# A table of slots in a fused Mamba and mixture-of-experts layer: softplus one slot earlier, normalisation three earlier, the first expert tile's Y one later

## The chip, the cores and the metric

The kernel runs on one core of a Trainium2 chip. The core has five engines that each work through a list of instructions in order: TensorE (PE) multiplies matrices, VectorE (DVE), ScalarE (ACT) and GpSimd (POOL) work on elements, SyncE (SP) issues DMAs. They wait for one another by semaphores. The metric is the time of one execution on the device in microseconds (us).

## The reference, cut to what matters

The input x has 2 batches of 4096 tokens of width 256. Everything is float32.

```python
xn = layernorm(x)
# Mamba branch
r = xn * rsqrt(mean(xn * xn) + eps) * norm_w
x_s, z = split(r @ in_proj_w.T)                  # 512 channels each
u = silu(causal_conv(x_s, 4 taps) + conv_b)
dt, B, C = split(u @ x_proj_w.T)                 # 16, 16, 16
delta = softplus(dt @ dt_proj_w.T + dt_proj_b)
h[t] = exp(delta[t] * A) * h[t-1] + delta[t] * u[t] * B[t]    # 512 channels x 16 states
y = (sum over states of h * C + u * D) * silu(z)
mamba = y @ out_proj_w.T + xn
# experts: 8, two per token
w = sparse_mixer_top2(xn @ gate_w.T)
moe = sum over chosen e of w_e * ((silu(xn @ w1[e].T) * (xn @ w3[e].T)) @ w2[e].T)
out = x + mamba + moe
```

## The kernel before, in words

The tokens are cut into 32 blocks of 256, ordered by `number(j, b)`, batch 0 and 1 in turn, since the recurrence runs along a batch. One block is worked in 32 slots, `v` = 0 to 31, one for each pair of a state and a half of the channels. In every slot the engines do the following.

- POOL makes the product du * B for the slot four ahead (`make_dbu`, L475) into a ring `h` of 8 buffers. It waits until PE has transposed what was in the buffer.
- ACT makes DA = exp(delta * A) for the next slot (`make_da`, L748), two ACTIVATEs, into a PSUM tile with two buffers. So it cannot run more than two slots ahead of the scans.
- DVE runs the recurrence as two scans (`scan`, L1071), waiting for both.
- PE transposes the state of two slots before (`transpose_h`, L1305) into HT, which has two halves, so that it waits for the addition of the state before the last. DVE multiplies by C and adds it (`add_state`, L1082), four slots behind the scan.

Around this carousel stand the steps that prepare the next block and finish the one before. The table `SLOTS` says in which slot each stands; every engine walks the same 32 slots and emits the steps that are due, in the order in which its `step` function asks for them. In one slot ACT emits DA first, then the steps of expert tiles, then tanh of z, the normalisation, and so on to exp and ln. The softplus is abs (L716), exp (L722) and ln (L730) on ACT, the sums `sp0`, `sp1` on DVE (L1061), and on POOL w-1 (`wm`, L483), the correction (`corr`, L488), `delta` (L494) and `du` (L499). ACT loads a table ahead of ln and another behind it. The first DA of the next block waits for `delta`, the first product for `du`. POOL waits for the exponential (`exp_ready`) at the start of the slot of `wm`, ahead of the product of that slot.

The experts' work comes in tiles of 128 token places that share an expert, 135 in all, in the blocks 2 to 28 at 5 a block. A tile starts at the slots 4, 13, 18, 23 and 30 (`XT_UNITS`); the stages after it are offsets: transposition XT, its copy on ACT, H1 = x w1 (L1354), H3 = x w3 (L1361), tanh on ACT (L647), the product A2 on DVE (L1038), MULT with H3 on DVE (L1047), Y = ha w2 (L1368) on PE, YO on ACT (L654), and on POOL the gather of a tile (L443) and the scatter of its result (L452), both indirect DMAs. `tile_of` turns a slot into a tile.

Of the kernel before, what the change touches and what calls it, by code (L numbers as in the profile page):

```python
# [27 lines left out]
def build(nc, x, norm_w, inT_d, conv_w, conv_b, xpT_d, dtT_d, dt_b, A_log, D_par, outT_d, gwT_d, w1T_d, w2T_d, w3T_d, out):  # L28
# [12 lines left out]
    U = CH * NS // 2  # L41
# [24 lines left out]
    with ExitStack() as ctx:  # L66
        def sb(name, shape, dt=F32):
            return ctx.enter_context(nc.sbuf_tensor(name, shape, dt))
# [60 lines left out]
        delta = sb("delta", [P, 2, CH, T])  # L129
        du = sb("du", [P, 2, CH, T])  # L130
# [6 lines left out]
        cT = sb("cT", [P, 2, NT, NS])  # L137
# [100 lines left out]
        def tile_of(j, b, v, stage):  # L238

            for k in range(PER):  # L240
                at = U * (k // len(XT_UNITS)) + XT_UNITS[k % len(XT_UNITS)] + stage
                for pair in (0, 1, -1):
                    if at - 2 * U * pair == U * b + v:
                        return j - pair, k
            return None

        def tiles_at(j, b, v, stage):

            at = tile_of(j, b, v, stage)
            if at is None:  # L250
                return None
            jj, k = at
            if isinstance(jj, int) and not (J0 <= jj and (jj - J0) * PER + k < NTILES):
                return None
            return (jj - J0) * PER + k, k

        def filled(j, b, v, stage, ring=WSLOTS):

            jj, k = tile_of(j, b, v, stage)
            return (jj - J0) * (PER // ring) + k // ring + 1  # L260
# [3 lines left out]
        def add_slot(j, b, v):  # L264
# [2 lines left out]
            return at // 2 if at >= 0 and at % 2 == 0 and at // 2 < 2 * JB - 2 else None  # L267

        SLOTS = {"z0": 31, "tanh_z0": 0, "silu_z0": 1, "z1": 2, "tanh_z1": 3, "silu_z1": 4,
                 "first0": 3, "first1": 4, "y0": 4, "gate_y0": 6, "y1": 5, "gate_y1": 7, "out0": 27, "out1": 29,  # L270
                 "oacc": 17, "result": 31,
# [4 lines left out]
        XT_UNITS = (4, 13, 18, 23, 30)  # L276

        LOGITS, ROUTE = 2, 3
# [5 lines left out]
            return isinstance(j, int) and number(j, b) == 1  # L284

        INDEX, GATHER = -5, -4
        XT, XT_COPY, H1, H3, TANH, A2, MULT, Y, YO, SCATTER = 0, 1, 2, 3, 3, 4, 4, 5, 6, 8
        W1_LOAD, W3_LOAD, W2_LOAD = 4, 5, 7

        def due(name, v):  # L290
# [1193 lines left out]
```

How the kernel before makes its waits and increments, by code:

```python
def wait(eng, sem, value):  # L17
    if not isinstance(value, int) or value > 0:
        eng.wait_ge(sem, value)
# [278 lines left out]
            def load_x(j, b):  # L299
                n = number(j, b)
                sp.wait_ge(s_inT, 16)
                if isinstance(n, int) and n < 3:
                    wait(sp, s_xn, 2 * n)
                else:
                    sp.wait_ge(s_res, n - 2)
                sp.dma_start(xraw[:, :, :], x_v[b, j]).then_inc(s_x, 16)
# [1 line left out]
            def reload_x(j, b):  # L308
                n = number(j, b)
                sp.wait_ge(s_inT, 16)
                if isinstance(n, int) and n + 2 >= 2 * JB:
                    sp.wait_ge(s_res, n)
                else:
                    sp.wait_ge(s_xn, 2 * (n + 2) + 2)
                sp.dma_start(xraw[:, :, :], x_v[b, j]).then_inc(s_xres, 16)
# [1 line left out]
            def store_b(j, b):  # L318
                n = number(j, b)
                sp.wait_ge(s_xdbc, n + 1)
                sp.dma_start(b_dram[b], xdbc[R:R + NS, :]).then_inc(s_bst, 16)
# [1 line left out]
            def load_b(j, b, r):  # L323
                n = number(j, b)
                if r == 0:
                    sp.wait_ge(s_bst, 16 * (n + 1))
                wait(sp, s_dbu, 32 * n + 4 * (r + 1 - BRING))
                sp.dma_start(bbc[:, r % BRING], b_dram[b][2 * r:2 * r + 2, :].partition_broadcast(P)).then_inc(s_b[r % BRING], 16)
# [1 line left out]
            def store_out(j, b):  # L330
                sp.wait_ge(s_res, number(j, b) + 1)
                sp.dma_start(out_v[b, j], res).then_inc(s_mamba, 16)
```

## Time and profile before

| | us |
|---|---|
| median of 3 runs | 2661.89 |
| lowest, highest | 2659.11, 2669.71 |
| the profiled execution, its own time | 2653.93 |
| its span in the trace | 2652.2 |
| share busy: DVE, PE, POOL, ACT | 93%, 86%, 77%, 63% |
| mean granted clock of TensorE | 0.936 |

The span is the time from the first to the last record of the trace. The stretch from about 400 to 2400 us holds the blocks with expert tiles, and one block there looks like the next. A row of a view in order of time has the start, the duration, the engine, the line, the operation, its tiles and how many instructions were merged; what stands in brackets is how long the engine had been idle and what ended it. A scan of a slot is two instructions. In such a view the slots are found by the steps that stand in them: the A2 of a tile that starts at 18 stands in slot 22.

### The profile page before, as it was taken

The page shows a single profiled execution, that of the slowest core. Times are in us where ns is not written, and L with a number is a line of the kernel's source. Part 1 is how long each engine was busy: PE and PEld are TensorE (multiplying, and loading weights), DVE is VectorE, ACT ScalarE, POOL GpSimd, SP SyncE. Part 2 cuts the span into 40 slices and gives each one's busy share as a digit, 9 for nine tenths or more (in the row PEclk, how much of TensorE's full clock was granted, in tenths as well). Part 3 has the DMA queues.
Part 4 walks back from the last instruction along what each step waited for, and adds up shares of the span by engine and source line. Part 5 has one row for each costly group of instructions (what it writes and reads, how often), then busy time and mean ns, then how long its engine had stood idle before and what let it go on. Part 6 is the DMA issues. An engine that isn't in the chain of part 4 may idle for free. (4 is left out here: it accounts for less than half of the span.)

```text
span 2652.2 us, 47132 instructions
## 1 busy us (share of the span) xinstructions
PE 2292.8 (86%) x14442; PEld 1986.7 (75%) x14442; DVE 2459.2 (93%) x4041; ACT 1658.9 (63%) x4137; POOL 2031.0 (77%) x1607
## 2 busy tenths in 40 slices
PE   3958789899999999998999989999989899998665
PEld 2855578878787887877888877888877787887554
DVE  7679999999999999999999999999999999999997
ACT  3940566666666666666666666666666666666653
POOL 3430678888888888888888888888888888888883
PEclk7858899999999999999999999999999999999776
DMA  7216045565555555555555555555555555542451
GB/s 244 92 40 216 29 124 156 154 176 152 161 151 152 157 160 171 158 157 153 155 160 155 166 163 151 158 156 160 154 162 164 156 152 157 159 113 52 96 100 32
DMA packets 267099, 379.38 MB, mean 143 GB/s; under 512 B 21492, under 2 KB 158324, under 8 KB 266852
## 3 DMA queue, kind: packets, MB, share of 16 engines
q1 hardware_dynamic: 236196, 332.26, 40.2%
q0 software_dynamic: 28480, 43.94, 10.1%
q8 instruction: 119, 1.95, 0.3%
q14 instruction: 128, 1.05, 0.1%
q10 hardware_dynamic: 2176, 0.18, 0.1%
HBM read 332.59 MB, written 52.10 MB: 145 GB/s over the span
## 5 line engine op out<-in xcount | busy, mean ns | idle before, releaser
L475 POOL TENSOR_TENSOR h<-du,bbc 128x512 f32<-128x512 f32 x1024 | 1362.5, 1354 | 505.3 <-PE HT L1305 375.3
L1071 DVE TENSOR_TENSOR_SCAN h<-DA,carry,h 128x256 f32<-128x256 f32 x2048 | 1417.7, 734 | 91.4 <-ACT DA L748 79.0
L748 ACT ACTIVATE DA<-delta,alog 128x256 f32<-128x256 f32 x2048 | 882.6, 468 | 212.2 <-DVE h L1071 200.9
L1305 PE MATMUL HT<-ident,h 128*128 128x128 f32 x4096 | 665.8, 288 | 260.5 <-DVE yT L1082 259.1
L1305 PEld LDWEIGHTS HT<-ident,h 128*128 128x128 f32 x4096 | 496.6, 148 | 416.2 <-issue 375.2
L1082 DVE SCALAR_TENSOR_TENSOR yT<-HT,cT,yT 128x512 f32<-128x512 f32 x960 | 698.5, 728 | 3.1 <-PE HT L1305 3.1
L1354 PE MATMUL G<-xtT,W 128*128 128x128 f32 x2160 | 273.2, 281 | 0.0
L1368 PE MATMUL G<-W,fill 128*128 128x256 f32 x1080 | 271.8, 397 | 0.0
L1361 PE MATMUL G<-xtT,W 128*128 128x128 f32 x2160 | 263.4, 275 | 0.0
L1354 PEld LDWEIGHTS G<-xtT,W 128*128 128x128 f32 x2160 | 261.1, 198 | 0.0
L1361 PEld LDWEIGHTS G<-xtT,W 128*128 128x128 f32 x2160 | 252.2, 192 | 0.0
L452 POOL DMA_INDIRECT moe_dram<-W,token x135 | 217.5, 1611 | 25.2 <-issue 24.3
L1368 PEld LDWEIGHTS G<-W,fill 128*128 128x128 f32 x1080 | 205.5, 201 | 24.7
L647 ACT ACTIVATE fill<-G 128x512 f32<-128x512 f32 x135 | 80.6, 597 | 190.7 <-PE G L1354 184.6
L443 POOL DMA_INDIRECT W<-xn_dram,token x135 | 139.7, 1035 | 21.8 <-issue 16.0
L483 POOL TENSOR_SCALAR tmpA<-tmpB 128x1024 f32<-128x1024 f32 x32 | 117.2, 3663 | 30.2 <-ACT tmpB L722 30.2
L654 ACT ACTIVATE W<-G,weight 128x256 f32<-128x256 f32 x135 | 63.7, 472 | 121.0 <-PE G L1368 120.9
L1226 PE MATMUL FA<-xrT,inT 128*128 128x256 f32 x512 | 128.2, 396 | 0.0
L1378 PE MATMUL FA<-outT,zs 128*128 128x256 f32 x512 | 127.2, 394 | 0.8 <-DVE zs L1098 0.8
L1226 PE MATMUL FB<-xrT,inT 128*128 128x256 f32 x512 | 126.4, 392 | 0.8 <-ACT xrT L617 0.8
L1047 DVE TENSOR_TENSOR fill<-fill,G 128x512 f32<-128x512 f32 x135 | 92.5, 685 | 36.7 <-PE G L1361 34.4
L1260 PE MATMUL FB<-xs,cwd 128*128 128x256 f32 x512 | 121.0, 379 | 0.0
(183 smaller groups left out, 2986.6 us busy)
## 6 DMA issues: line engine op xcount, KB each, us to landing
W<-in_w_T_dram SPq DMA_DIRECT2D x405, 512.0 KB, 4.2
bbc<-b_dram SPq DMA_DIRECT2D x256, 256.0 KB, 4.3
xraw<-in_x_dram SPq DMA_DIRECT2D x64, 256.0 KB, 2.7
xn_dram<-W SPq DMA_DIRECT2D x8, 1032.0 KB, 14.0
W<-in_x_dram SPq DMA_DIRECT2D x32, 256.0 KB, 6.7
moe_dram<-fill SPq DMA_DIRECT2D x32, 256.0 KB, 4.0
out_dram<-tmpA SPq DMA_DIRECT2D x32, 256.0 KB, 2.2
out_dram<-moe_dram POOLq DMA_DIRECT2D x32, 256.0 KB, 4.4
```

Of the source, the lines that this page charges most:

```text
L443: pool.indirect_dma_start(xt[:, k % 2, :], None, xn_dram[:, :], bass.IndirectOffsetOnAxis(ap=token[:, k % META:k % META + 1], axis=0)).the ...
L452: pool.indirect_dma_start(moe_dram[:, :], bass.IndirectOffsetOnAxis(ap=token[:, k % META:k % META + 1], axis=0), yo[:, k % 2, :], None, co ...
L475: pool.tensor_tensor(h[:, v % RING], du[:, b, 2 * q:2 * q + 2, :], bbc[:, s // 2 % BRING, s % 2, :].unsqueeze(1).to_broadcast([P, 2, T]), ...
L748: i = act.activation(DA[:, v % 2, k, :], delta[:, b, c, :], ACT.Exp, scale=nega[:, c, s:s + 1])
L1071: i = dve.tensor_tensor_scan(h[:, v % RING, k, :], DA[:, v % 2, k, :], h[:, v % RING, k, :], carry[:, b, s, c:c + 1], ALU.mult, ALU.add)
L1082: i = dve.scalar_tensor_tensor(out=yT[:, b, k, :], in0=HT[:, k, :], scalar=cT[:, b, k, s:s + 1], in1=yT[:, b, k, :], op0=ALU.mult, op1=ALU ...
L1226: i = pe.matmul(dst[:, c, :], inT[:, k, at:at + P], xrT[:, b, k, :], start=(c == 0 and k == 0), stop=(k == KD - 1), skip_group_check=True)
L1305: i = pe.transpose(HT[:, k, c * P:(c + 1) * P], h[:, (2 * s + c // 2) % RING, c % 2, k * P:(k + 1) * P], ident[:, :])
L1354: i = pe.matmul(G[:, 0, f * P:(f + 1) * P], w1[:, k % WSLOTS, c, f * P:(f + 1) * P], xtT[:, c, :], start=(f == 0 and c == 0), stop=(c == K ...
L1361: i = pe.matmul(G[:, 1, f * P:(f + 1) * P], w3[:, k % WSLOTS, c, f * P:(f + 1) * P], xtT[:, c, :], start=(f == 0 and c == 0), stop=(c == K ...
L1368: i = pe.matmul(G[:, 0, 0:DM], ha[:, f * P:(f + 1) * P], w2[:, k % WSLOTS, f, :], start=(f == 0), stop=(f == IC - 1))
L1378: i = pe.matmul(FA[:, t, :], zs[:, c, t * P:(t + 1) * P], outT[:, c, :], start=(c == 0), stop=(c == CH - 1))
```

## The change

In the table `SLOTS` the exponential goes from slot 22 to 21 and the logarithm from 23 to 22; `sp0`, `sp1`, `wm`, `corr`, `delta`, `du`, `cT` and `copy_cT` go one slot up as well. The normalisation of the next block goes from 6 to 3, the second product of the input projection from 10 to 9, the second half of the output projection from 29 to 28, the result from 31 to 30. Of the expert tiles, MULT, Y and YO become offsets for each of the five tiles: the tile that starts at 4 has its MULT at 9 in place of 8, its Y at 10 in place of 9 and its YO at 11 in place of 10; the tile that starts at 23 has its Y at 29 and its YO at 30, one later each. All scatters stand one slot later. `tile_of` gets a line that takes such a tuple.

```diff
-                at = U * (k // len(XT_UNITS)) + XT_UNITS[k % len(XT_UNITS)] + stage
+                at = U * (k // len(XT_UNITS)) + XT_UNITS[k % len(XT_UNITS)]
+                at += stage[k % len(XT_UNITS)] if isinstance(stage, tuple) else stage
...
-                 "x_proj": 17, "copy_xdbc": 18, "dt": 19, "abs": 20, "exp": 22, "ln": 23, "sp0": 24, "sp1": 25,
-                 "wm": 23, "corr": 24, "delta": 26, "du": 27, "cT": 25, "copy_cT": 26}
+                 "x_proj": 17, "copy_xdbc": 18, "dt": 19, "abs": 20, "exp": 21, "ln": 22, "sp0": 23, "sp1": 24,
+                 "wm": 22, "corr": 23, "delta": 25, "du": 26, "cT": 24, "copy_cT": 25}
...
-        XT, XT_COPY, H1, H3, TANH, A2, MULT, Y, YO, SCATTER = 0, 1, 2, 3, 3, 4, 4, 5, 6, 8
+        XT, XT_COPY, H1, H3, TANH, A2, SCATTER = 0, 1, 2, 3, 3, 4, 9
+        MULT, Y, YO = (5, 4, 4, 4, 4), (6, 5, 5, 6, 5), (7, 6, 6, 7, 6)
```

The lines of the changed kernel are numbered two higher behind these. On ACT, from slot 21 to slot 24, `fill<-G` is the tanh of a tile, `tmpB<-tmpA` the exponential, `xs<-tmpB` the logarithm. Before:

```order
L748 ACTIVATE DA<-delta,alog 128x256 x2
L647 ACTIVATE fill<-G 128x512
L748 ACTIVATE DA<-delta,alog 128x256 x2
L755 COPY carry<-h 128x4
L722 ACTIVATE tmpB<-tmpA 128x1024
L748 ACTIVATE DA<-delta,alog 128x256 x2
L730 ACT_TABLE_LOAD
L730 ACTIVATE xs<-tmpB 128x4x256
L748 ACT_TABLE_LOAD
L748 ACTIVATE DA<-delta,alog 128x256 x2
```

The same stretch of ACT in the changed kernel:

```order
L750 ACTIVATE DA<-delta,alog 128x256 x2
L649 ACTIVATE fill<-G 128x512
L724 ACTIVATE tmpB<-tmpA 128x1024
L750 ACTIVATE DA<-delta,alog 128x256 x2
L757 COPY carry<-h 128x4
L732 ACT_TABLE_LOAD
L732 ACTIVATE xs<-tmpB 128x4x256
L750 ACT_TABLE_LOAD
L750 ACTIVATE DA<-delta,alog 128x256 x4
```

Two DAs stood between the tanh and the first table load and one does now; the DAs for scans 24 and 25 both stand behind the second load.

On POOL, from the slot of `wm` to the start of the next block, `h<-du,bbc` is a product for a slot four ahead, `W<-xn_dram` a gather, `moe_dram<-W` a scatter. Before:

```order
L483 TENSOR_SCALAR tmpA<-tmpB 128x1024
L475 TENSOR_TENSOR h<-du,bbc 128x512
L488 TENSOR_TENSOR tmpA<-tmpB,tmpA 128x1024
L475 TENSOR_TENSOR h<-du,bbc 128x512
L430 COPY token<-W 128x1
L475 TENSOR_TENSOR h<-du,bbc 128x512
L494 TENSOR_TENSOR delta<-delta,tmpA 128x1024
L443 DMA W<-xn_dram,token 128x258
L452 DMA moe_dram<-W,token 8320x256
L475 TENSOR_TENSOR h<-du,bbc 128x512
L499 TENSOR_TENSOR du<-delta,u 128x1024
L475 TENSOR_TENSOR h<-du,bbc 128x512 x4
```

The changed kernel, from the row behind its w-1 (now L485):

```order
L454 DMA moe_dram<-W,token 8320x256
L477 TENSOR_TENSOR h<-du,bbc 128x512
L490 TENSOR_TENSOR tmpA<-tmpB,tmpA 128x1024
L477 TENSOR_TENSOR h<-du,bbc 128x512 x2
L496 TENSOR_TENSOR delta<-delta,tmpA 128x1024
L432 COPY token<-W 128x1
L477 TENSOR_TENSOR h<-du,bbc 128x512
L501 TENSOR_TENSOR du<-delta,u 128x1024
L445 DMA W<-xn_dram,token 128x258
L477 TENSOR_TENSOR h<-du,bbc 128x512
L454 DMA moe_dram<-W,token 8320x256
L477 TENSOR_TENSOR h<-du,bbc 128x512 x4
```

Both lists end with the first four products of the next block. Between w-1 and these stand 4 products and one scatter before, and 5 products and two scatters now. The wait for the exponential stands one product ahead of w-1 in both: before, the product for slot 27, and now, that for slot 26.

On DVE, in slots 8 and 9, `fill<-fill,G` is A2 (L1038) and MULT (L1047) of the tile that starts at 4. Before:

```order
L1071 SCALAR_TENSOR_TENSOR h<-DA,carry,h 128x256 x2
L1038 SCALAR_TENSOR_TENSOR fill<-fill,G 128x512
L1082 SCALAR_TENSOR_TENSOR yT<-HT,cT,yT 128x512
L1047 TENSOR_TENSOR fill<-fill,G 128x512
L1071 SCALAR_TENSOR_TENSOR h<-DA,carry,h 128x256 x2
L1082 SCALAR_TENSOR_TENSOR yT<-HT,cT,yT 128x512
```

And in the changed kernel:

```order
L1073 SCALAR_TENSOR_TENSOR h<-DA,carry,h 128x256 x2
L1040 SCALAR_TENSOR_TENSOR fill<-fill,G 128x512
L1084 SCALAR_TENSOR_TENSOR yT<-HT,cT,yT 128x512
L1073 SCALAR_TENSOR_TENSOR h<-DA,carry,h 128x256 x2
L1084 SCALAR_TENSOR_TENSOR yT<-HT,cT,yT 128x512
L1049 TENSOR_TENSOR fill<-fill,G 128x512
```

MULT stands behind the scan and the addition of slot 9.

## Rows read from the trace of the kernel before

**Rows 1.** The page: busy time of each engine, share, instructions.
```profile
PE 2292.8 (86%) x14442; PEld 1986.7 (75%) x14442; DVE 2459.2 (93%) x4041; ACT 1658.9 (63%) x4137; POOL 2031.0 (77%) x1607
```

**Rows 2.** Waits of DVE, 800 to 2300 us: total us, times, longest us.
```profile
DVE h L1071 <- ACT DA L748: 28.7, 58, 0.6
DVE fill L1047 <- PE G L1361: 24.2, 62, 1.3
...
DVE h L1071 <- POOL h L475: 2.9, 14, 0.2
```

**Rows 3.** DVE in order of time: start, duration; in brackets the wait before.
```profile
1002.02 1.39 DVE L1071 TENSOR_TENSOR_SCAN h<-DA,carry,h 128x256 f32<-128x256 f32 x2 [0.45 <-ACT DA L748]
...
1005.83 1.39 DVE L1071 TENSOR_TENSOR_SCAN h<-DA,carry,h 128x256 f32<-128x256 f32 x2
1007.13 0.72 DVE L1082 SCALAR_TENSOR_TENSOR yT<-HT,cT,yT 128x512 f32<-128x512 f32 x1
1007.77 1.38 DVE L1071 TENSOR_TENSOR_SCAN h<-DA,carry,h 128x256 f32<-128x256 f32 x2
...
1010.79 1.39 DVE L1071 TENSOR_TENSOR_SCAN h<-DA,carry,h 128x256 f32<-128x256 f32 x2 [0.40 <-ACT DA L748]
...
1027.32 1.39 DVE L1071 TENSOR_TENSOR_SCAN h<-DA,carry,h 128x256 f32<-128x256 f32 x2 [0.19 <-POOL h L475]
...
1040.79 1.39 DVE L1071 TENSOR_TENSOR_SCAN h<-DA,carry,h 128x256 f32<-128x256 f32 x2 [0.64 <-ACT DA L748]
...
1049.01 0.69 DVE L1047 TENSOR_TENSOR fill<-fill,G 128x512 f32<-128x512 f32 x1 [0.51 <-PE G L1361]
...
1078.82 1.39 DVE L1071 TENSOR_TENSOR_SCAN h<-DA,carry,h 128x256 f32<-128x256 f32 x2 [0.45 <-ACT DA L748]
```

**Rows 4.** ACT in order of time, slots 21 to 24.
```profile
1003.00 0.60 ACT L647 ACTIVATE fill<-G 128x512 f32<-128x512 f32 x1 [1.01 <-PE G L1354]
...
1004.38 1.06 ACT L722 ACTIVATE tmpB<-tmpA 128x1024 f32<-128x1024 f32 x1
1005.34 0.86 ACT L748 ACTIVATE DA<-delta,alog 128x256 f32<-128x256 f32 x2
...
1009.89 0.87 ACT L748 ACTIVATE DA<-delta,alog 128x256 f32<-128x256 f32 x2
```

**Rows 5.** POOL in order of time, slots 26 to 8.
```profile
1019.27 1.06 POOL L443 DMA_INDIRECT W<-xn_dram,token  x1
...
1022.95 2.92 POOL L499 TENSOR_TENSOR du<-delta,u 128x1024 f32<-128x1024 f32 x1
1025.95 4.96 POOL L475 TENSOR_TENSOR h<-du,bbc 128x512 f32<-128x512 f32 x4
...
1042.56 1.27 POOL L475 TENSOR_TENSOR h<-du,bbc 128x512 f32<-128x512 f32 x1 [1.09 <-ACT carry L755]
...
1045.05 3.08 POOL L475 TENSOR_TENSOR h<-du,bbc 128x512 f32<-128x512 f32 x2
```

**Rows 6.** ACT in order of time, slots 4 and 6.
```profile
1039.52 0.47 ACT L654 ACTIVATE W<-G,weight 128x256 f32<-128x256 f32 x1 [0.48 <-PE G L1368]
...
1042.46 1.09 ACT L601 ACTIVATE tmpA<-xraw,nrs,rs 128x256 f32<-128x256 f32 x2
```

**Rows 7.** Chain of waits, slots 9 to 17: start, duration, piece.
```profile
2209.23 0.44 PE HT L1305 x4
2209.67 1.73 PE FA L1226 x8
...
2222.94 1.80 PE G L1361 x16
```

**Rows 8.** PE in order of time, slot 23.
```profile
1008.00 0.63 PE L1305 MATMUL HT<-ident,h 128*128 128x128 f32 x4 [2.25 <-DVE yT L1082]
```

**Rows 9.** One stretch: busy us (instructions) of PE, PEld, DVE, ACT, POOL; clock, DMA.
```profile
1009.00:1012.00 3.00, 3.00 (x11) 2.37 (x10) 2.60 (x5) 2.96 (x8) 3.00 (x3) 0.55 0.12 46
```

**Rows 10.** DVE in order of time, slot 27 of another block.
```profile
2249.57 0.69 DVE L1038 SCALAR_TENSOR_TENSOR fill<-fill,G 128x512 f32<-128x512 f32 x1 [1.02 <-ACT fill L647]
```

More of the change, by code:

```diff
@@ L269, in build @@
         SLOTS = {"z0": 31, "tanh_z0": 0, "silu_z0": 1, "z1": 2, "tanh_z1": 3, "silu_z1": 4,
-                 "first0": 3, "first1": 4, "y0": 4, "gate_y0": 6, "y1": 5, "gate_y1": 7, "out0": 27, "out1": 29,
-                 "oacc": 17, "result": 31,
[1 row of a table removed]
+                 "first0": 3, "first1": 4, "y0": 4, "gate_y0": 6, "y1": 5, "gate_y1": 7, "out0": 27, "out1": 28,
+                 "oacc": 17, "result": 30,
[1 row of a table added]
                  "conv0": 11, "conv1": 12, "conv2": 13, "conv3": 14, "tanh_u0": 13, "silu_u0": 14, "tanh_u1": 15, "silu_u1": 16,
[2 rows of a table removed]
[2 rows of a table added]
         XT_UNITS = (4, 13, 18, 23, 30)
```

2 rows, old and new, of the table SLOTS are left out of this document.

## The prediction

> **What bounds the kernel now.** I read the page first: DVE is busy for 93% of the span, POOL for 77%, PE for 86% [rows 1]. Busy shares do not say who is late, so next came the waits of DVE in the steady stretch, 800 to 2300 us, about 19.5 blocks: scans wait for the exponentials DA of ACT (28.7 us), the third product of an expert tile waits for PE's H3 (24.2 us), and scans wait for POOL's products only 2.9 us [rows 2]. Then I read one block in order of time. DVE starts slot 22 at 1002.02 and the next slot 22 at 1078.82, so a block lasts 76.8 us, and the reader is to see where DVE waits in it: 0.45 at scan 22, 0.40 at scan 25, 0.19 at scan 0, 0.64 at scan 6, 0.51 for H3 in slot 8 [rows 3]. These and a few smaller gaps sum to some 4 us, so a change of order can win at most about 5%.
>
> The small wait at scan 0 is the important one. It shows that POOL, though 77% busy, has no slack there: from the exponential of the softplus to the first product of the next block it works without a pause. The chain of waits says a third thing: from slot 9 to slot 17 PE is continuously busy and DVE waits for its last piece, H3 [rows 7]. So three engines take turns within one block: ACT at slots 22 to 25, POOL from there to slot 0, PE from slot 3 to slot 17. A term counts only where its engine has the turn.
>
> **The exponential and logarithm one slot earlier: ACT.** In the profile ACT works without a pause from the tanh at 1003.00 to the end of DA 25 at 1009.89 + 0.87 = 1010.76: tanh, DA 23, exp, DA 24, table load, ln, table load, DA 25 [rows 4]. The new order does the same work: tanh, exp, DA 23, load, ln, load, DA 24, DA 25. DA 25 is ready at 1010.76 again, but DA 24 only 0.87 before, at 1009.9, where it was ready at about 1006.2 before. DA has two buffers, so it cannot be made earlier. DVE wants scan 24 after scan 23 (1005.83 to 1007.13), a state addition (to 1007.77) [rows 3] and the first softplus sum, which now stands there and which I put at the 0.65 of the addition: 1008.4. The wait is 1.5 us in place of the 0.40 at scan 25, so DVE is 1.1 us late from here on. In slot 27 H3 comes relatively 0.3 later, since the second softplus sum no longer separates scans 25 and 26, and at scan 0 the old 0.2 of waiting is used up. On DVE's own path scan 0 comes 1.2 us late, at 1028.5.
>
> **The same steps on POOL.** POOL's w-1, correction, delta and du move one slot up, the scatters of the expert tiles one slot down. From the end of the exponential to the end of the product for scan 0, POOL had 6 products and one scatter beside these four passes, one gather and one token copy. In the new order the wait for the exponential stands ahead of the product for scan 26, and the scatter that was issued before that wait comes behind it, while the second scatter still precedes the product for scan 0. So 7 products and two scatters lie between. Prices: a product takes 4.96 / 4 = 1.24 us [rows 5]. A scatter: between the end of a product at 42.56 + 1.27 = 43.83 and the end of the second next at 45.05 + 3.08 = 48.13 lie 4.30 us, less two products 1.8 us. The other end is from the gather's end at 19.27 + 1.06 = 20.33 to the start of du at 22.95: 2.62 less one product, 1.4 us [rows 5]. Added work is 1.24 + 1.4 to 1.8; the exponential ends 0.87 earlier, since DA 23 no longer stands ahead of it. The product for scan 0 is ready 1.8 to 2.2 us later than 25.95 + 1.24 = 1027.19, at 1029.0 to 1029.4. That is behind the 1028.5 of DVE's own path, so POOL decides, and scan 0 starts 1.75 to 2.15 us later than in [rows 3]. I take 1.9. Behind it POOL has pauses and catches up. The gather for the fourth tile now starts behind du, at about 1024; it has to land by about 1027.6, so PE may wait some tenths there, which slot 31 hides.
>
> **Normalisation at 3.** Two ACTIVATEs, 1.09 us, move from behind DA 7 to ahead of DA 5. Scan 6 waits for DA 6 already [rows 3], and between the old and the new place of the step ACT waits only 0.48 us, for PE, ahead of YO [rows 6]. So DA 6, and with it scan 6, comes 1.09 - 0.48 = 0.6 us later. Removing it from slot 6 gives nothing, since ACT then waits for H1 anyhow.
>
> **First tile's product at 9, Y at 10.** The product ha no longer waits in slot 8: 0.51 us less on DVE. That the two do not simply add comes from PE. Its work of slots 3 to 8 depends on DVE's slot 3 and runs on. The state addition of slot 9, which releases PE's slot 9, is then about 0.5 us earlier than now; that of slot 10, which now comes behind the moved product, is back where it was (0.6 later by the normalisation, 0.5 earlier by the wait). From slot 10 on PE has the same matmuls as before (the xs product and Y swap), each with its transposes about 2.17 us [rows 7], against 1.95 of DVE. So PE reaches H3 of slot 17 within about 0.1 of where it does now. I count zero for both edits, with -0.5 and +0.6 as ends, where only one of them reaches the end. YO one slot later lies just ahead of DA 13, which is ready at 1057.5 where scan 13 wants it at 1057.6: cover is used up but nothing is lost.
>
> **Output at 28, result at 30, cT at 24, other scatters.** PE's slots 27 to 29 exchange out and Y, with room. SP's stores come one slot earlier. Zero, covered by PE's waits for state additions in slots 30 and 31.
>
> **The sum.** 135 tiles at 5 a block lie in 27 blocks: 27 x 1.9 = 51.3. The 4 other blocks with a successor have no scatters, so only ACT's 1.1 counts: 4.4. Together 55.7 us. The profiled execution took 2653.93 (span 2652.2), so it would be 2709.6; it was 8 us faster than the median of the runs, 2661.89, so for the median 2717.6.
>
> **Rivals.** (a) The clock falls once more per block. In the profile PE pauses 2.25 us before slot 23 [rows 8], and in the stretch behind it, 1009 to 1012, the granted clock is 0.55, so most of it ran at 1.2 of 2.4 GHz [rows 9]; there it costs nothing. In one block it fell later, under the first product of the tile at 23, and that tile's A2 waited 1.02 us [rows 10]; slot 27 in other blocks had no such wait. In the new order scan 24 comes 1.5 us later, so PE, which waits for the state addition behind each scan, pauses before slots 24 and 25 too, about 1 us more in all. The Trainium skill, "TensorE: Matmul & The Clock Gate", section "Part 1: The HAM clock gate", says that the array falls to 1.2 GHz after idling and returns to 2.4 GHz under sustained work; by that rule the added pause speaks for a fall at this second place, and the trace agrees as far as its one late case goes. Price: DVE's path reaches scan 0 at 1028.5 + 1.0 = 1029.5 plus up to 0.6 from H3; that is 0.3 to 0.9 behind POOL, so 2.2 to 2.8 a block, 2726 to 2742. With part of the 0.6 of the normalisation on top it is 2750. Chance 0.22. (b) The 0.5 of the moved product is kept and scatters overlap the products: 0.7 to 1.4 a block, 2685 to 2704. Chance 0.14. (c) The other side: ACT. If ACT could run ahead by 1.6 us, DA 24 would be ready by 1008.4, and the early exponential would give POOL its 0.87 while the waits of 0.40, 0.19 and 0.51 went. That is 1.1 a block, 31 us: 2631. It decides at the tanh of slot 21: it would have to start before 1001.4, but PE's H1 ends at 1003.0 and POOL must have no second scatter in the way. Chance 0.08. (d) The terms cancel, within 0.5% (about 13 us, what a measurement of this kernel can tell from no change): it needs POOL's prices to be wrong, spans there being rough, and the 0.5 to be kept. 2662, chance 0.08. My forecast has the remaining 0.48.
>
> **Numbers.** Slower: forecast, (a) and (b), 0.48 + 0.22 + 0.14 = 0.84. Same 0.08, faster 0.08. The range leaves out (c) and (d) and runs from the low end of (b), 2685, to the high end of (a), 2750.
>
> **What would show it.** Scan 24 waits about 1.5 us for DA, the wait at scan 25 is gone; scan 0 waits 0.5 to 0.9 us for POOL, and the total of DVE's waits for POOL rises from 2.9 us to over 10. The H3 wait in slot 8 is gone. A block lasts 78.7 us in place of 76.8. I would be wrong if the scan 24 wait were under 0.5 us, if scan 0 did not wait for POOL, or if the block lasted 77 us or less.

## The result, and the profile after

| | before | after |
|---|---|---|
| median, us (4 runs each) | 2664.3 | 2727.36 |
| lowest, highest | 2659.11, 2669.71 | 2724.11, 2731.28 |
| profiled execution, its span | 2653.93, 2652.2 | 2731.28, 2729.5 |
| mean granted clock of TensorE | 0.936 | 0.918 |

The changed kernel takes 1.0237 [1.0211, 1.0264] of the time, 63 us more. The forecast was 2718 with a range of 2685 to 2750. The time is inside it, but a good part of it came by another road than the forecast said: 2727 also lies in the 2726 to 2742 that I gave rival (a), the clock, and it is this rival that the profile shows at work.

The page after, to be laid beside [rows 1]. DVE works as long as before (2457 and 2459 us) in a span 77 us longer, so all of the loss is waiting; PE shows 41 us more work for the same number of instructions.

```profile
PE 2333.5 (85%) x14442; PEld 2032.4 (74%) x14442; DVE 2457.1 (90%) x4041; ACT 1658.8 (61%) x4137; POOL 2026.6 (74%) x1607
```

The waits of DVE, 800 to 2300 us (total us, times, longest), beside [rows 2]:

```profile
DVE h L1073 <- ACT DA L750: 42.9, 74, 1.5
DVE fill L1040 <- ACT fill L649: 34.4, 37, 2.1
DVE fill L1049 <- PE G L1363: 22.2, 71, 0.9
DVE h L1073 <- issue: 9.0, 6, 1.5
```

And one row of the kernel before, for the same window:

```profile
DVE fill L1038 <- ACT fill L647: 6.4, 24, 1.0
```

Three things are to be seen. The longest wait for DA is now 1.5, as forecast; the last row is the same wait at scan 24, in six blocks in which the profile names nobody for it. The second row is a wait that the forecast had only as a rival: A2, which waits for ACT's tanh of an expert tile, rose from 6.4 us (24 times, longest 1.0) to 34.4 us. And there is no row for POOL at all, where the forecast had over 10 us.

One block of the changed kernel on DVE, in order of time (start, duration, in brackets the wait ahead), beside [rows 3]: scan 22, scan 24, then slot 27's A2 and product, scan 0, scans 5 and 6, slot 9's product of the first tile, scan 22 of the next block, its scan 24 and its A2, and the scan 0 behind that.

```profile
1028.79 1.39 DVE L1073 TENSOR_TENSOR_SCAN h<-DA,carry,h 128x256 f32<-128x256 f32 x2 [0.45 <-ACT DA L750]
...
1036.78 1.39 DVE L1073 TENSOR_TENSOR_SCAN h<-DA,carry,h 128x256 f32<-128x256 f32 x2 [1.50 <-ACT DA L750]
...
1046.67 0.69 DVE L1040 SCALAR_TENSOR_TENSOR fill<-fill,G 128x512 f32<-128x512 f32 x1 [2.08 <-ACT fill L649]
...
1048.91 0.69 DVE L1049 TENSOR_TENSOR fill<-fill,G 128x512 f32<-128x512 f32 x1 [0.89 <-PE G L1363]
...
1057.88 1.38 DVE L1073 TENSOR_TENSOR_SCAN h<-DA,carry,h 128x256 f32<-128x256 f32 x2
...
1069.89 1.39 DVE L1073 TENSOR_TENSOR_SCAN h<-DA,carry,h 128x256 f32<-128x256 f32 x2 [0.43 <-ACT DA L750]
1071.72 1.39 DVE L1073 TENSOR_TENSOR_SCAN h<-DA,carry,h 128x256 f32<-128x256 f32 x2 [0.44 <-ACT DA L750]
...
1081.30 0.67 DVE L1049 TENSOR_TENSOR fill<-fill,G 128x512 f32<-128x512 f32 x1
...
1108.92 1.39 DVE L1073 TENSOR_TENSOR_SCAN h<-DA,carry,h 128x256 f32<-128x256 f32 x2 [0.45 <-ACT DA L750]
...
1116.91 1.39 DVE L1073 TENSOR_TENSOR_SCAN h<-DA,carry,h 128x256 f32<-128x256 f32 x2 [1.50 <-ACT DA L750]
...
1126.19 0.69 DVE L1040 SCALAR_TENSOR_TENSOR fill<-fill,G 128x512 f32<-128x512 f32 x1 [1.46 <-ACT fill L649]
...
1136.92 1.38 DVE L1073 TENSOR_TENSOR_SCAN h<-DA,carry,h 128x256 f32<-128x256 f32 x2
```

From scan 22 to scan 0 it takes 29.09 us here and 28.00 in the next block, where it took 25.30 [rows 3]: +3.8 and +2.7. (Over all blocks it goes in turn 28.0, 27.7, 29.1, 28.0.) From scan 0 to the next scan 22 it takes 51.04 in place of 51.50: 0.46 less. Scan 24 waits its 1.50 and scan 25 no longer waits. Slot 9's product does not wait. Scan 0 does not wait for POOL: DVE itself comes too late for that.

What made A2 late stands on PE, slots 23 to 25, in order of time (the last row is H1 of the tile that starts at 23):

```profile
1034.77 0.63 PE L1307 MATMUL HT<-ident,h 128*128 128x128 f32 x4 [2.25 <-DVE yT L1084]
...
1038.96 0.63 PE L1307 MATMUL HT<-ident,h 128*128 128x128 f32 x4 [1.61 <-DVE yT L1084]
...
1041.50 1.09 PE L1307 MATMUL HT<-ident,h 128*128 128x128 f32 x4 [1.66 <-DVE yT L1084]
1042.38 3.62 PE L1356 MATMUL G<-xtT,W 128*128 128x128 f32 x16
```

And the same stretch in windows of 3 us (busy us and instructions of PE, PEld, DVE, ACT, POOL; then the granted clock; DMA share and GB/s):

```profile
1036.00:1039.00 3.00, 1.39 (x8) 0.91 (x7) 2.22 (x4) 2.97 (x10) 2.84 (x4) 1.00 0.35 45
1039.00:1042.00 3.00, 1.34 (x9) 1.07 (x10) 3.00 (x6) 1.85 (x6) 3.00 (x3) 0.73 0.82 212
1042.00:1045.00 3.00, 3.00 (x16) 3.00 (x15) 2.59 (x5) 0.00 (x0) 3.00 (x3) 0.50 0.00 0
1045.00:1048.00 3.00, 3.00 (x19) 3.00 (x19) 1.33 (x2) 1.96 (x5) 2.92 (x4) 0.63 0.21 35
1048.00:1051.00 3.00, 3.00 (x20) 2.48 (x19) 2.11 (x5) 0.38 (x3) 2.85 (x2) 1.00 0.88 281
```

For comparison the same transposes of slot 25 and the same H1 in the kernel before:

```profile
1012.98 0.63 PE L1305 MATMUL HT<-ident,h 128*128 128x128 f32 x4 [0.44 <-DVE yT L1082]
1013.44 1.95 PE L1354 MATMUL G<-xtT,W 128*128 128x128 f32 x16
```

The pause of 2.25 ahead of slot 23 stood there before [rows 8]. Ahead of slot 24 there was none and is 1.61 now, ahead of slot 25 there was 0.44 and is 1.66 now. Both are the echo of scan 24's wait, since PE's transposes wait for the state addition that follows a scan. (In two of four blocks the clock has fallen already behind the pause of 2.25; the slower work then fills the pause ahead of slot 24, the 1.66 stays, and the clock is down a second time under H1.) The clock falls between 1039 and 1042 (0.73 in that window), is at 0.50, half of 2.4 GHz, up to 1045 and back at 1.00 from 1048, and H1 takes 3.62 us, where it takes 1.95 at full clock. The tanh and A2 hang on that H1. Over 420 to 2400 us the mean granted clock fell from 0.98 to 0.96; I estimate from these figures about 79 us at half speed before (twice 0.02 of 1980) and about 158 after.

The kernel before has a fall of the clock in most blocks too, but mostly ahead of H1, where it costs nothing [rows 9]. In 8 of its 27 blocks with tiles it comes late and lies under H1, and there it takes 26.5 to 26.7 us from scan 22 to scan 0 in place of 25.3.

POOL after, from the exponential to the product for scan 0:

```profile
1031.39 1.28 POOL L477 TENSOR_TENSOR h<-du,bbc 128x512 f32<-128x512 f32 x1 [3.36 <-ACT tmpB L724]
...
1036.44 1.65 POOL L454 DMA_INDIRECT moe_dram<-W,token  x1 [0.16 <-issue]
...
1052.92 1.62 POOL L454 DMA_INDIRECT moe_dram<-W,token  x1 [0.17 <-issue]
1054.00 5.51 POOL L477 TENSOR_TENSOR h<-du,bbc 128x512 f32<-128x512 f32 x4
```

As forecast, POOL waits for the exponential ahead of a product and then has two scatters on its way. The product for scan 0 starts 25.2 us behind scan 22, where it started 1025.95 - 1002.02 = 23.9 behind it [rows 3, 5], and it is slower for the scatter beside it. But DVE arrives 29.09 behind scan 22, when it has been ready for some 2 us. The forecast's deciding wait is there and hidden under a larger one.

To compare kernels below I give the block: the distance between two starts of the addition that makes the result (DVE, L1108 in the kernel before), one per block, as a mean of 26 blocks. Before it is 77.18 (most blocks 76.8, those with a late fall of the clock 78.0 to 78.8), after 79.34 (in turn 79.03, 79.10, 78.87 and 80.44). That is 26 x 2.16 = 56 us; of the remaining 21 us between the two profiled executions, 11 lie ahead of the first addition counted here, the second of the kernel (409.36 and 420.47), and 10 in the last blocks. The kernel before is not even in its blocks, the changed one is worse.

### The profile page after: what moved, and what is told of

Its sections match the earlier page's. It is cut to its first block and busy times, and to the rows that moved or that the text cites. A ratio compares the mean times of both kernels' runs of the same rounds, so it can differ in the third digit from the quotient of the medians.

```text
span 2729.5 us, 47131 instructions
## 1 busy us (share of the span) xinstructions
PE 2333.5 (85%) x14442; PEld 2032.4 (74%) x14442; DVE 2457.1 (90%) x4041; ACT 1658.8 (61%) x4137; POOL 2026.6 (74%) x1607
## 3 DMA queue, kind: packets, MB, share of 16 engines
q8 instruction: 119, 1.95, 0.3%
## 5 line engine op out<-in xcount | busy, mean ns | idle before, releaser
L1307 PE MATMUL HT<-ident,h 128*128 128x128 f32 x4096 | 676.6, 292 | 296.4 <-DVE yT L1084 296.0
L1307 PEld LDWEIGHTS HT<-ident,h 128*128 128x128 f32 x4096 | 504.9, 150 | 444.4 <-issue 405.7
L1356 PE MATMUL G<-xtT,W 128*128 128x128 f32 x2160 | 299.8, 299 | 0.0
L1356 PEld LDWEIGHTS G<-xtT,W 128*128 128x128 f32 x2160 | 289.0, 215 | 0.0
L1363 PE MATMUL G<-xtT,W 128*128 128x128 f32 x2160 | 265.1, 276 | 0.0
L1363 PEld LDWEIGHTS G<-xtT,W 128*128 128x128 f32 x2160 | 254.3, 193 | 0.0
L485 POOL TENSOR_SCALAR tmpA<-tmpB 128x1024 f32<-128x1024 f32 x32 | 116.6, 3645 | 30.7 <-ACT tmpB L724 30.7
L1040 DVE SCALAR_TENSOR_TENSOR fill<-fill,G 128x512 f32<-128x512 f32 x135 | 91.1, 675 | 50.1 <-ACT fill L649 50.1
```

The lines of the kernel that those rows point to most:

```text
L1307: i = pe.transpose(HT[:, k, c * P:(c + 1) * P], h[:, (2 * s + c // 2) % RING, c % 2, k * P:(k + 1) * P], ident[:, :])
L1356: i = pe.matmul(G[:, 0, f * P:(f + 1) * P], w1[:, k % WSLOTS, c, f * P:(f + 1) * P], xtT[:, c, :], start=(f == 0 and c == 0), stop=(c == K ...
L1363: i = pe.matmul(G[:, 1, f * P:(f + 1) * P], w3[:, k % WSLOTS, c, f * P:(f + 1) * P], xtT[:, c, :], start=(f == 0 and c == 0), stop=(c == K ...
```

## The experiments

Two explanations stand against each other: my forecast (ACT at scan 24, then POOL decides scan 0), and rival (a), the clock under the tile's H1. The expectations below letter their theories anew for each run. Ratios are to the kernel before on the same chip (medians 2659.19, 2661.61 and 2663.67 in three batches), with their 95% interval.

### The softplus group alone

```diff
-  "abs": 20, "exp": 22, "ln": 23, "sp0": 24, "sp1": 25,
-  "wm": 23, "corr": 24, "delta": 26, "du": 27, "cT": 25, "copy_cT": 26}
+  "abs": 20, "exp": 21, "ln": 22, "sp0": 23, "sp1": 24,
+  "wm": 22, "corr": 23, "delta": 25, "du": 26, "cT": 24, "copy_cT": 25}
```

> The kernel before with only the softplus group one slot up (exp 21, ln 22, sp, wm, corr, delta, du, cT); scatters stay at 8, everything else as before. Theory A (the group alone costs: DA 24 is 1.1 us late, and PE's added pauses of about 1.6 us before slots 24 and 25 let the clock fall under H1 of the tile at 23): a block takes 78.5 to 79.4 us, scan 24 waits 1.5 us for DA, A2 of slot 27 waits 1 to 2 us; ratio to before 1.020 to 1.025, nearly all of the change. Theory B (POOL decides, by the second scatter between exponential and du, as my prediction had it): here one scatter less lies in POOL's chain, so scan 0 is only 1.2 us late, ratio 1.013.

Measured: 2730.57, ratio 1.026 [1.0237, 1.0282], block 79.90. Its waits have the same shape as those of the changed kernel:

```profile
DVE h L1071 <- ACT DA L748: 47.1, 56, 1.5
DVE fill L1038 <- ACT fill L647: 36.9, 37, 2.1
DVE fill L1047 <- PE G L1361: 28.4, 75, 1.0
```

The group makes the whole loss and slightly more; the rest of the change gives a little back. Here the scatters stay where they were, so POOL has one scatter less on its way to scan 0; if POOL decided, the ratio would have been near 1.013. It is 1.026, and no scan waits for POOL between 800 and 2300 us. So in this kernel it is not POOL that decides.

### The change without the softplus group, with and without the later scatters

`e2_rest_only` has all of the change but the group above; `e12_rest_scatter8` is the same with the scatters where they were:

```diff
-        XT, XT_COPY, H1, H3, TANH, A2, SCATTER = 0, 1, 2, 3, 3, 4, 9
+        XT, XT_COPY, H1, H3, TANH, A2, SCATTER = 0, 1, 2, 3, 3, 4, 8
```

> The changed kernel with the softplus group back at its old slots: normalisation at 3, xs1 at 9, output 27 and 28, result 30, first tile's MULT, Y, YO one later, fourth tile's Y and YO one later, scatters at 9. Theory A (all these cost nothing in sum): ratio 0.998 to 1.002, the 0.51 us wait for H3 in slot 8 gone, scan 6 about 0.6 us later, PE's chain of slots 9 to 17 where it was. Theory C (the normalisation's 0.6 us a block reaches the end): ratio 1.006. Theory D (the 0.5 us of the moved product is kept): ratio 0.995.

> The changed kernel without the softplus group and with the scatters back at offset 8; what is left is normalisation, xs1, output, result, first and fourth tile. Theory A (scatters at 9 put one between the transposed state and the exponential on POOL, which showed as 1.07 us of waiting at scan 0 in place of 0.2): that wait goes, 0.4 to 0.9 us a block less than with the scatters at 9, ratio 0.994 to 0.998. Rival: the same ratio as with them, 1.0025.

Measured: 2668.24, ratio 1.0025 [1.001, 1.004], against 2655.62, ratio 0.9974 [0.9957, 0.9991]. One row of DVE in the first, scan 0 of a block:

```profile
1104.76 1.39 DVE L1073 TENSOR_TENSOR_SCAN h<-DA,carry,h 128x256 f32<-128x256 f32 x2 [1.08 <-POOL h L477]
```

Scan 0 waits 1.08 for POOL, where it waited 0.19 [rows 3]. DVE's waits for POOL between 800 and 2300 us sum to 11.5 us in the first and 1.1 in the second. POOL in the first, from slot 22 to the product for scan 0 (its scan 22 starts at 1078.59):

```profile
1081.64 1.63 POOL L454 DMA_INDIRECT moe_dram<-W,token  x1 [0.16 <-issue]
...
1083.95 4.23 POOL L485 TENSOR_SCALAR tmpA<-tmpB 128x1024 f32<-128x1024 f32 x1
...
1101.71 1.63 POOL L454 DMA_INDIRECT moe_dram<-W,token  x1 [0.17 <-issue]
```

Between w-1 and scan 0's product both kernels have one scatter, so it is not a matter of one more. Two places count. One scatter now stands ahead of w-1, which starts 5.36 us behind scan 22 in place of 4.72. The other now stands behind `du`, right ahead of the product for scan 0, and that product takes 1.84 us in place of 1.27. In all scan 0 comes 26.17 behind scan 22 in place of 25.30, wherever the clock has not fallen late. By the medians the later scatters cost about 13 us in this kernel; I had priced the other scatters at nothing.

### Keeping TensorE busy: after, and before

The transposes of slots 22, 23 and 24 are repeated 5, 4 and 5 times. They write the same values to the same place, so the results and the order of the steps stay; PE is busy where it paused. (In the code `u` is the slot whose scan is transposed, two behind; the dots stand for indices that do not change.)

```diff
-                for c in range(CH):
-                    i = pe.transpose(HT[:, k, ...], h[...], ident[:, :])
+                for _ in range({20: 5, 21: 4, 22: 5}.get(u, 1)):
+                    for c in range(CH):
+                        i = pe.transpose(HT[:, k, ...], h[...], ident[:, :])
```

> The changed kernel with PE's pauses filled: the four transposes of the state are done 5, 4 and 5 times over in slots 22, 23 and 24 (the same values again), so PE is busy where it paused 2.25, 1.6 and 1.7 us. Theory A (the fall of the clock adds to the loss): H1 of the tile at 23 takes 1.95 us in place of 3.6, A2 of slot 27 waits under 0.3 us, and now POOL decides: scan 0 waits 0.4 to 0.9 us for POOL, a block 78.7 us, ratio to before 1.018 to 1.020, 10 to 16 us under the changed kernel. Rival: A2 waits because PE comes late to H1 and not because it runs slowly: no gain over the changed kernel, ratio 1.024.

> The kernel before with the same filling. Theory A: there the fall of the clock costs only in the blocks where it comes late (8 of 27, 78.0 to 78.8 us against 76.8), so a block goes from 77.2 to 76.8 us on average, ratio 0.995 to 0.997. Rival: the repeated transposes hold up the state additions or Y, ratio 1.003 or more.

The changed kernel with it: 2691.43, ratio 1.0119 [1.0096, 1.0142], 36 us faster than without (31 by the two ratios, each taken to the kernel before in its own batch). Every block lasts 78.2. PE, slots 24 and 25, in order of time:

```profile
1015.15 2.37 PE L1308 MATMUL HT<-ident,h 128*128 128x128 f32 x20 [0.31 <-DVE yT L1084]
...
1018.20 1.95 PE L1357 MATMUL G<-xtT,W 128*128 128x128 f32 x16
```

The same block on DVE, scans 22, 24, 0 and the next 22:

```profile
1004.98 1.39 DVE L1073 TENSOR_TENSOR_SCAN h<-DA,carry,h 128x256 f32<-128x256 f32 x2 [0.45 <-ACT DA L750]
...
1012.97 1.39 DVE L1073 TENSOR_TENSOR_SCAN h<-DA,carry,h 128x256 f32<-128x256 f32 x2 [1.49 <-ACT DA L750]
...
1032.15 1.39 DVE L1073 TENSOR_TENSOR_SCAN h<-DA,carry,h 128x256 f32<-128x256 f32 x2 [0.68 <-POOL h L477]
...
1083.21 1.39 DVE L1073 TENSOR_TENSOR_SCAN h<-DA,carry,h 128x256 f32<-128x256 f32 x2 [0.45 <-ACT DA L750]
```

And its waits, 800 to 2300 us:

```profile
DVE h L1073 <- ACT DA L750: 52.6, 76, 1.5
DVE fill L1049 <- PE G L1364: 14.0, 57, 0.2
DVE h L1073 <- POOL h L477: 12.7, 19, 0.7
DVE fill L1040 <- ACT fill L649: 4.1, 19, 0.2
```

The window 420 to 2400 us has a granted clock of 1.00, H1 takes 1.95, and A2 no longer waits (34.4 to 4.1 us). Scan 24 still waits 1.49, and now scan 0 waits 0.68 for POOL, 12.7 us in all. From scan 22 to scan 0 it takes 27.17, which is 1.87 over 25.30 [rows 3]: the forecast's 1.9, in a kernel with the clock kept up. From scan 0 to the next scan 22 it takes 51.06, 0.44 less than before. So both explanations hold in part. ACT and POOL make the +1.9 once the clock is kept up; in the changed kernel as it stands the clock comes on top of ACT's part and covers POOL's.

The kernel before with the same filling: 2670.66, ratio 1.0023 [1.0004, 1.0042], all blocks but one 77.42. I had expected a gain. DVE in slot 27 shows why there is none:

```profile
1026.58 0.69 DVE L1038 SCALAR_TENSOR_TENSOR fill<-fill,G 128x512 f32<-128x512 f32 x1 [0.30 <-ACT fill L647]
...
1028.57 0.69 DVE L1047 TENSOR_TENSOR fill<-fill,G 128x512 f32<-128x512 f32 x1 [0.64 <-PE G L1362]
```

The kernel before lacks the wait at scan 24, so PE has no pause ahead of slot 24 once the one ahead of slot 23 is filled. The 16 transposes in slot 23 and the 20 in slot 24 push the rest of PE's list back, and H1 and H3 come late: A2 waits 0.30 in every block, and the product with H3 0.64 in the one shown. A filler must be no longer than the pause.

### POOL's part again, with the clock kept up

The changed kernel with the repetitions (`e3_after_busy`), and in it the scatters back at 8:

```diff
-        XT, XT_COPY, H1, H3, TANH, A2, SCATTER = 0, 1, 2, 3, 3, 4, 9
+        XT, XT_COPY, H1, H3, TANH, A2, SCATTER = 0, 1, 2, 3, 3, 4, 8
```

> The changed kernel with PE's pauses filled (5, 4, 5 times the transposes in slots 22 to 24) and the scatters back at offset 8. Theory A (with the clock up POOL decides at scan 0, and a scatter costs it 1.4 to 1.8 us): the wait of 0.7 us for POOL at scan 0 goes, a block 77.5 us in place of 78.2, ratio to before 1.003 to 1.006. Rival (not the scatter but the order of du and the products decides): scan 0 still waits, block 78.2, ratio 1.012.

Measured: 2663.59, ratio 1.0018 [0.9994, 1.0041], every block 77.45, no wait for POOL. So one scatter fewer ahead of scan 0 is worth 78.23 - 77.45 = 0.78 a block, about what separated POOL's product from DVE's own path in the forecast (1.9 against 1.2). On POOL the scatter is worth more: from the start of w-1 to the start of scan 0's product it takes 21.40 us with two scatters and 19.75 with one, 1.65 less, inside the forecast's 1.4 to 1.8. DVE's own path takes over before that is used up. It is ACT's part alone: scan 24 waits 1.50, and from scan 22 to scan 0 it takes 26.41, 1.1 over 25.30 (forecast 1.2). The kernel before with the same repetitions has nearly the same block, 77.42, but by another road: there H1 comes late and scan 24 does not wait.

### The normalisation alone

```diff
-                 "normalise": 6, "transpose": 7,
+                 "normalise": 3, "transpose": 7,
```

> The kernel before with the normalisation at slot 3 alone. Theory A: scan 6 comes 0.4 to 0.6 us later, but DVE waits for H3 in slot 8 anyhow (0.51 us), so that wait takes it up: block unchanged, ratio 0.999 to 1.002. Theory C (it reaches the end): 0.4 to 0.6 us a block, ratio 1.005.

Measured: 2667.81, ratio 1.0013 [0.9991, 1.0035]. It costs nothing that can be measured. Counted from scan 0, scan 5 comes 0.57 us later than in the kernel before and scans 6 to 8 come 0.39 later; at scan 9 nothing is left of it (22.28 in place of 22.29), since the wait for H3 in slot 8 takes it up.

### The first tile's product, without and with the projection

The first kernel moves MULT, Y and YO of the tile that starts at 4 one slot later and nothing else. The second moves the second product of the input projection from 10 to 9 as well, as the change does.

```diff
-        XT, XT_COPY, H1, H3, TANH, A2, MULT, Y, YO, SCATTER = 0, 1, 2, 3, 3, 4, 4, 5, 6, 8
+        XT, XT_COPY, H1, H3, TANH, A2, MULT, Y, YO, SCATTER = 0, 1, 2, 3, 3, 4, (5, 4, 4, 4, 4), (6, 5, 5, 5, 5), (7, 6, 6, 6, 6), 8
```

In the second kernel also, with the rest of the line cut:

```diff
-                 ... "xs1": 10, ...
+                 ... "xs1": 9, ...
```

> The kernel before with MULT, Y and YO of the tile at 4 one slot later, all else as before. Theory A (learned from the changed kernel with PE kept busy, whose stretch from scan 0 to scan 22 is 51.06 us against 51.50): the 0.51 us wait for H3 in slot 8 goes, PE's slot 9 starts so much earlier, 0.4 to 0.5 us a block is kept, ratio 0.994 to 0.997. My prediction's view (PE's chain to slot 17 takes it back): ratio 1.000.

> The kernel before with the first tile's MULT, Y, YO one slot later and the second xs product at slot 9 in place of 10, so that it fills PE's slot 9 which Y left. Theory A (in the run with the first tile alone Y and xs stood both in PE's slot 10, behind an empty slot 9 with a pause of 1.55 us; the two moves belong together): a block takes 0.4 to 0.5 us less than before where the clock stays up, 76.4 against 76.8, ratio 0.994 to 0.998. Rival (the one slot later is what costs): 77.4 us and 1.011 as with the first tile alone.

The first missed: 2692.71, ratio 1.0115 [1.0088, 1.0142], where I expected a small gain. PE, slot 10, in order of time:

```profile
1069.29 0.63 PE L1306 MATMUL HT<-ident,h 128*128 128x128 f32 x4 [1.55 <-DVE yT L1083]
1069.76 1.89 PE L1369 MATMUL G<-W,fill 128*128 128x256 f32 x8
1071.49 1.89 PE L1227 MATMUL FA<-xrT,inT 128*128 128x256 f32 x8
```

Slot 9 has only its transposes left and PE pauses 1.55 us ahead of slot 10, which has both Y and the projection. PE has no time to spare from slot 9 to 17 [rows 7], so the pause is paid at the end of that chain: DVE's `u` (L1055), which waits for ACT's tanh of the convolution, has 14.9 us of waits (19 times, longest 0.8). From scan 0 to scan 22 it takes 52.39 us in place of 51.50, +0.89. The block grew by more, 78.5 against 77.2; the rest lies between scan 22 and scan 0, where the late fall of the clock now comes in 17 of the blocks and not in 8.

With the projection at 9 the same move gives 2642.12, ratio 0.9923 [0.9894, 0.9951], and 50.77 from scan 0 to scan 22. What made the gain is one row of PE, slot 9. First in the kernel before (scan 0 at 1027.32), then in the second kernel (scan 0 at 1023.06):

```profile
1051.79 0.63 PE L1305 MATMUL HT<-ident,h 128*128 128x128 f32 x4 [0.65 <-DVE yT L1082]
```

```profile
1046.70 0.60 PE L1306 MATMUL HT<-ident,h 128*128 128x128 f32 x4
```

Before, PE paused 0.65 us there for DVE's addition of slot 9. The moved product and its wait no longer stand ahead of that addition, so PE starts slot 9 at 23.64 behind scan 0 in place of 24.47, and its chain to slot 17 ends 0.73 earlier. The swap is the point: this is kept only if something else fills PE's slot 9.

### One pause filled of three

The first kernel of the last section, with the transposes of slot 22 alone repeated 5 times (the lines inside the loop as above):

```diff
+                for _ in range({20: 5}.get(u, 1)):
```

> A candidate: the kernel before with MULT, Y and YO of the tile at 4 one slot later, and the transposes of slot 22 alone done 5 times, which fills PE's pause of 2.25 us and leaves slots 23 and 24 as they are (the filling of all three cost 0.6 us a block on the kernel before: H1 came later). Theory A: no fall of the clock, no late block, 76.4 us in every block against 77.2 on average, ratio 0.990 to 0.993. Rival: one filled pause does not keep the clock up, ratio as with the first tile alone, 0.995.

Measured: 2693.75, ratio 1.0124 [1.0098, 1.0151], as without the filling. PE around slot 25:

```profile
1022.17 0.63 PE L1307 MATMUL HT<-ident,h 128*128 128x128 f32 x4 [1.96 <-DVE yT L1083]
1022.63 3.46 PE L1356 MATMUL G<-xtT,W 128*128 128x128 f32 x16
```

With the pause ahead of slot 23 filled (0.50 is left), the product Y behind it runs at full clock, 1.89 us in place of the 2.99 of the kernel before, PE is through sooner, and the pause ahead of slot 25 is 1.96, where it was 0.44 in the kernel before. The clock falls behind that one, and H1 takes 3.46 us. This late fall comes in 15 of the blocks, where it came in 17; in the others the same two pauses, 0.50 and 1.96, stand ahead of an H1 of 1.95, and what else decides is not shown. Filling the longest pause alone does not remove the late fall. Since the clock still fell, this run does not tell what the clock costs in this kernel. That the move is slow by itself shows in the stretch from scan 0 to scan 22, with 52.39 us in both.

### The version that the experiments point to

The kernel before, with the first tile's product and the projection moved, and the transposes of slot 22 repeated 5 times and of slot 24 three times. Beside it the kernel before with these repetitions alone.

```diff
-                 ... "xs1": 10, ...
+                 ... "xs1": 9, ...
...
-        XT, XT_COPY, H1, H3, TANH, A2, MULT, Y, YO, SCATTER = 0, 1, 2, 3, 3, 4, 4, 5, 6, 8
+        XT, XT_COPY, H1, H3, TANH, A2, MULT, Y, YO, SCATTER = 0, 1, 2, 3, 3, 4, (5, 4, 4, 4, 4), (6, 5, 5, 5, 5), (7, 6, 6, 6, 6), 8
...
+                for _ in range({20: 5, 22: 3}.get(u, 1)):
```

> The same with the transposes of slot 22 done 5 times and those of slot 24 done 3 times. Theory A (the clock falls because of the pauses around slots 23 and 25 together, and filling slot 23 and 24 fully was what delayed H1): no fall of the clock, 76.4 us in every block, ratio 0.988 to 0.992. Rival (any filling delays H1 or the pause left at slot 23 lets the clock fall): ratio 0.995 or more.

> The kernel before with this smaller filling (slot 22 five times, slot 24 three times) and nothing else. Theory A: no fall of the clock, 76.8 us in every block against 77.2 on average, ratio 0.994 to 0.997. Rival: H1 is delayed again, 77.4 us a block, 1.002.

Measured: 2632.3, ratio 0.9882 [0.9856, 0.9909], a block 76.19 on average; and 2650.29, ratio 0.9952 [0.9929, 0.9975], a block 76.87. In both the clock stays at 1.00 between 420 and 2400 us. The first is 31 us faster than the kernel before and 95 faster than the change. With none in slot 23 and three in place of five in slot 24 the filler gives the gain that `e4_before_busy` spent again; which of the two differences does it was not taken apart. The two parts nearly add: 0.9923 x 0.9952 = 0.9875.

## Why the prediction was right, and where it was not

- **ACT.** Right. Scan 24 waits 1.50 (forecast 1.5), scan 25 no longer waits, and with POOL and the clock out of the way scan 0 comes 1.1 later (forecast 1.2).
- **POOL.** The step was right and not what decided. Its +1.9 is measured as +1.87 from scan 22 to scan 0, but only in `e3_after_busy`. In the changed kernel "POOL decides" is wrong: scan 0 does not wait for POOL in any block. The prediction had named just that as a sign that it would be wrong, and by this sign its account of the loss is wrong, though its time is right.
- **Rival (a), the clock.** This is what happened, in every block, not in some. I gave it 0.22. I had the pauses, but put them at about 1 us more in all; in the block shown they grew by 2.8, to 1.61 and 1.66 from 0 and 0.44. And I set against them one late case in [rows 10] and wrote that slot 27 in other blocks had no such wait. That was a misreading: the kernel before had the late fall in 8 of 27 blocks. The price was 2.2 to 2.8 a block; from scan 22 to scan 0 it was 2.4 to 3.8, since A2 waited 1.3 to 2.08 and not 1.0. By 77.18, 79.34 and 78.23 a block the changed kernel lost 2.16, of which 1.11 go when the clock is kept up.
- **Normalisation and the moved product, "zero for both".** This step of the sum failed. They bring 0.44 a block from scan 0 to scan 22 in `e3_after_busy`, and 0.1 to 0.46 in the changed kernel. I had argued that PE's chain to slot 17 takes the product's 0.5 back and ends within 0.1 of where it did. I had the addition of slot 9 come 0.5 earlier and forgot that the product itself, 0.69 us, goes out of its way too: scan 9 comes 1.2 earlier (21.09 behind scan 0 in place of 22.29). So PE's pause ahead of slot 9 goes, and with the projection there to fill the slot the chain ends 0.73 earlier (0.9923). Without it the move loses (1.0115). I had counted that swap as neutral. Scan 6's delay of 0.6 was about 0.4 (13.86 from scan 0 in `e3_after_busy`, 13.47 before). Alone it costs nothing (1.0013), because the wait for H3 takes it up; together with the swap, which removes that wait, it does cost: scan 9 comes 0.39 later than with the swap alone in `e12_rest_scatter8`, and the next scan 22 still 0.28 later (51.05 against 50.77). These two kernels differ in the output steps and in the fourth tile as well, but the 0.39 stands there from scan 6 on, right behind the moved normalisation.
- **The other scatters, "zero".** Wrong for the kernel without the softplus group (1.0025 against 0.9974) and part of POOL's term in the full one.
- **The sum.** +1.9 - 0.45 + 1.1 is 2.55 over an undisturbed block of 76.8, which is 79.35. It must come out near the measured 79.34, since the 1.1 is the difference of two measured blocks; it tells how the loss divides and is no test of it. Forecast: 78.7. Two errors of opposite sign, the clock left out (+1.1) and the swap left out (-0.45), and a third, the 1.9 counted from 76.8 where the average block before already had 77.18, brought the forecast within 10 us of the measured median. That is luck. A time inside the range says little of the steps.

Some things stay open. The first addition counted comes 11 us later in the changed kernel (420 and 409), and the last blocks take 10 us more. The clock alone does not explain the first: with the repetitions the changed kernel has 403 and 404, but `e2_rest_only` has 404 without any repetition and `e4_before_busy` 417 with them. Nor does it explain the last blocks, which take 236 us in `e3_after_busy`, as in the changed kernel (235), against 225 before. And why the blocks of one kernel differ in a fixed turn (79.03, 79.10, 78.87, 80.44) was not followed further than the length of A2's wait.

## What to carry to other kernels

Before a step is moved ahead of another on a full engine, follow the wait that it makes to the engines that wait for its victim: here 1.5 us on DVE became two pauses on PE, and these halved the clock under the next long product. To see what lies under such a wait, fill the pauses, and no more than the pauses, with repeated work that changes no result, and measure again. Two moves that look separate (the product to 9, the projection to 9) can be one swap, so take them apart in both directions before either is called neutral.

## What the runs showed of the hardware

In the changed kernel the granted clock fell to half between 1039 and 1042, after pauses of PE of 2.25 and 1.61 us and around one of 1.66, with PE busy in between, and came back while PE worked without a pause (the windows up to 1051). In the kernel before it fell behind the pause of 2.25 alone [rows 8, 9]. No pause of PE was longer than 2.25 us between 420 and 2400 us in either. 16 matmuls that take 1.95 us at 2.4 GHz took 3.62 us there. Repeating transposes of 0.6 us four or five times in these pauses kept the clock at 1.00 from 420 to 2400 us. With only the pause of 2.25 filled, one of 1.96 was followed by the slow H1 in 15 of 27 blocks and by an H1 at full clock in the others. An indirect scatter of 1.6 us on POOL also lengthens its neighbours: the product behind it ends 1.84 us after its start in place of 1.28, and so do the products that follow without a gap, though they still start 1.23 us apart (1054.00, 1055.23, 1056.46 and 1057.68 in the changed kernel).
